# Second attention: each head's stack on 64 partitions, one score matmul per head, one run for the value product

## The reference

```
loc_p   = softmax(Qb Kb^T / 4);                 out  = loc_p Vb
cross_p = softmax(Qb Kw^T / 4), Kw = own, left and right block;  out += cross_p Vw
```

## Time and profile before

| | |
|---|---|
| median of three runs | 1000.9 us |
| lowest, highest run | 999.47, 1026.03 us |
| span of the profiled execution | 999.6 us |
| mean granted clock of TensorE | 0.915 of 2.4 GHz |
| instructions | 15908 |
| busy: TensorE, VectorE, ScalarE, GpSimd | 852.5, 444.8, 351.0, 227.6 us |
| second attention | between 84 and 501 us, with attention 1 of batches 1 to 3 between the passes |
| experts | from about 530 us to the end |

### The profile page before, as it was taken

One profiled execution on the slowest core, in us unless ns is written; L12 is line 12 of the kernel. 1 busy time (PEld: TensorE's weight loads), 2 busy tenths in 40 slices (PEclk: granted clock), 3 DMA queues, 4 the chain that ended last, 5 costly groups with the idle time before them and its releaser, 6 DMA issues. The chain is left out here.

```text
span 999.6 us, 15908 instructions
## 1 busy us (share of the span) xinstructions
PE 852.5 (85%) x5062; PEld 643.2 (64%) x5063; DVE 444.8 (45%) x821; ACT 351.0 (35%) x902; POOL 227.6 (23%) x248
## 2 busy tenths in 40 slices
PE   3476779987997899799994999899999999999940
PEld 3365566766675757565674999767766677777630
DVE  5854537556756675544236655222222222222216
ACT  1210126442643354314515443033333333333313
POOL 6730203020302030000002577511111111111115
PEclk9687689989998899895897999999999999999975
DMA  9702120212021204120008211544111111111025
GB/s 306 127 0 66 50 57 4 60 53 61 4 58 48 66 0 129 34 55 1 4 1 314 103 53 53 142 167 135 31 37 31 31 31 31 37 31 32 26 73 196
DMA packets 59000, 68.48 MB, mean 69 GB/s; under 512 B 18160, under 2 KB 43632, under 8 KB 58832
## 3 DMA queue, kind: packets, MB, share of 16 engines
q1 hardware_dynamic: 55552, 58.61, 20.1%
q0 software_dynamic: 3408, 9.34, 2.6%
HBM read 38.23 MB, written 16.59 MB: 55 GB/s over the span
## 5 line engine op out<-in xcount | busy, mean ns | idle before, releaser
L1529 PE MATMUL ps<-we,hT 128*128 x624 | 142.8, 382 | 2.5 <-ACT hT L714 2.5
L1509 PE MATMUL ps<-we,xT 128*128 x312 | 142.3, 599 | 1.9 <-issue 1.9
L1529 PEld LDWEIGHTS ps<-we,hT 128*128 128x128 f32 x624 | 119.7, 192 | 35.5 <-issue 20.9
L918 DVE TENSOR_REDUCE mx<-ps 128x4 f32<-128x512 f32 (+1 forms) x128 | 102.9, 822 | 77.0 <-PE ps L1349 76.0
L1112 DVE COPY hp<-ps 128x512 f32<-128x512 f32 x78 | 50.3, 686 | 160.1 <-PE ps L1509 160.1
L714 ACT ACTIVATE hT<-ps,b1T 128x128 f32<-128x128 f32 x312 | 84.7, 383 | 37.2 <-PE ps L1520 37.2
L1509 PEld LDWEIGHTS ps<-we,xT 128*128 128x128 f32 x312 | 56.8, 192 | 59.2 <-issue 59.2
L1349 PE MATMUL ps<-k_stack,q_stack 96*128 96x256 f32 (+1 forms) x256 | 76.7, 389 | 18.7 <-DMA q_stack<-q_s 11.7
L617 ACT ACTIVATE pT<-ps 128x256 f32<-128x256 f32 x128 | 49.1, 384 | 107.9 <-PE ps L1364 100.3
L540 ACT ACTIVATE xT<-ps 128x256 f32<-128x256 f32 x39 | 14.8, 383 | 180.8 <-PE ps L1492 180.8
L1349 PEld LDWEIGHTS ps<-k_stack,q_stack 96*128 96x128 f32 x256 | 43.5, 212 | 52.6 <-issue 24.4
(11 more groups left out here) (202 smaller groups left out, 1339.1 us busy)
## 6 DMA issues: line engine op xcount, KB each, us to landing
we<-in_w SPq DMA_DIRECT2D x16, 1024.0 KB
k_stack<-k_s SPq DMA_DIRECT2D x96, 64.0 KB, 2.0
q_stack<-q_s SPq DMA_DIRECT2D x192, 32.0 KB, 2.0
slot_rows<-attn SPq DMA_DIRECT2D x1, 4992.0 KB, 21.2
xs<-slot_rows SPq DMA_DIRECT2D x39, 128.0 KB, 2.1
yl<-pair_out SPq DMA_DIRECT2D x4, 1024.0 KB, 9.2
x_raw<-in_xT SPq DMA_DIRECT2D x4, 512.0 KB, 3.9
X<-in_x SPq DMA_DIRECT2D x4, 512.0 KB, 7.2
```

The lines of the kernel that those rows point to most:

```text
L918: nc.vector.tensor_reduce(mx[:, n, 2 * p:2 * p + 2, r0:r0 + nb], ps[:, 2 * (u % 2):2 * (u % 2) + 2, 0:nb * P].rearrange("p h (b k) -> p h ...
L1509: m = nc.tensor.matmul(ps[:, 2 + c, :], xT[:, q, k, :], w[:, bass.ds(e, 1), k * HID + c * 512:k * HID + (c + 1) * 512].rearrange("p o n -> ...
L1529: m = nc.tensor.matmul(ps[:, 6, 0:D], hT[:, c, :], w[:, bass.ds(e, 1), KD * HID + c * D:KD * HID + (c + 1) * D].rearrange("p o n -> p (o n)"),
```

## The change

Each head gets a stack of its own of 64 partitions: head 0 of a pair stands on partitions 0 to 63, head 1 on 64 to 127. 48 rows hold the three products (16 each). Rows 48 to 55 hold the local difference, two rows for each of the four blocks, each filled for its own query block and zero elsewhere; `k_stack` has ones there only for the key block of the same number. Rows 56 and 57 hold the window's maximum against ones. So the right correction is added for local and side blocks by the same matmul, and for each head one matmul over the whole window (256 or 384 columns) takes the place of the shared local one and the shared sides one. The maxima matmuls contract 48 rows, the probability ones 58, in place of 96, 98 and 100.

`q_stack` has half the size. The columns of the query and key weights of attention 2 are reordered on the host, so that a copy takes 32 partitions of source into 16 partitions and two pairs: 12 issues of 64 KB for each of two groups of pairs, 24 for a half. TensorE waits for a group at every eighth unit, not for a pair at every fourth. `aug_rows` has 10 issues: for each head of a pair one for the window rows and four for the local ones. The fixed rows of `k_stack` come from a small tile `k_rows`, which GpSimd makes with a memset and two selects, by two DMAs at the start of SP's order; VectorE's memset goes.

The value product has one run of four matmuls for a block of keys, over its whole window, in odd units only. Even key blocks go to bank 7 and odd ones to bank 6, so that a query block's own part and its neighbours' part are in different banks; `turn_out` picks them accordingly. The exponentials have 256 or 384 columns each, one per head, and the second matmul of a unit waits for the second exponential of the unit before.

```diff
-PAIR_DMAS = 3 + 2 * 3
-
-
-def side_blocks(i):
-    return [n for n in (i - 1, i + 1) if 0 <= n < NT]
+GROUPS = 2
+GROUP_DMAS = 2 * 3 * 2
+ROWS_A = 3 * DH
+ROW_LOC = ROWS_A
+ROW_CROSS = ROW_LOC + 2 * NT
+ROWS_B = ROW_CROSS + 2
+AUG_DMAS = 2 + 2 * NT
+
+
+def window(i):
+    return max(i - 1, 0), 3 if 0 < i < NT - 1 else 2
...
-        q_stack = sb("q_stack", [P, HEADS, S], FR, att)
+        q_stack = sb("q_stack", [P, HEADS // 2, S], FR, att)
...
+            sp.wait_ge(s["k_set"], 3)
+            for j in range(2):
+                sp.dma_start(k_stack[64 * j + ROW_LOC:64 * j + ROWS_B, :, :].bitcast(F),
+                             k_rows[:, :].unsqueeze(1).broadcast_to([2 * NT + 2, HEADS // 2, S])).then_inc(s["k_ones"], 16)
...
-                for g in range(PAIRS):
-                    for sec, part in enumerate((0, 1, 0)):
-                        sp.dma_start(k_stack[32 * sec:32 * sec + 32, h * PAIRS + g, :].bitcast(F),
-                                     k_s[32 * g:32 * g + 32, h, part, :].bitcast(F)).then_inc(stacked[g], 16)
-                    for head in (2 * g, 2 * g + 1):
+                for g in range(GROUPS):
+                    pairs = slice(h * PAIRS + 2 * g, h * PAIRS + 2 * g + 2)
+                    for j in range(2):
+                        rows = slice(64 * j + 32 * g, 64 * j + 32 * g + 32)
+                        for sec, part in enumerate((0, 1, 0)):
+                            r = 64 * j + DH * sec
+                            sp.dma_start(k_stack[r:r + DH, pairs, :].bitcast(F),
+                                         k_s[rows, h, part, :].bitcast(F)).then_inc(stacked[g], 16)
                         for sec, part in enumerate((0, 0, 1)):
-                            r = 32 * sec + 16 * (head % 2)
-                            sp.dma_start(q_stack[r:r + 16, h * HALF + head, :].bitcast(F),
-                                         q_s[16 * head:16 * head + 16, h, part, :].bitcast(F)).then_inc(stacked[g], 16)
+                            r = 64 * j + DH * sec
+                            sp.dma_start(q_stack[r:r + DH, pairs, :].bitcast(F),
+                                         q_s[rows, h, part, :].bitcast(F)).then_inc(stacked[g], 16)
 
             def aug_rows(b, h):
                 sp.wait_ge(s["augT_out"], 2 * b + h + 1)
-                for r in range(4):
-                    sp.dma_start(q_stack[96 + r:97 + r, h * HALF:(h + 1) * HALF, :].bitcast(F),
-                                 augT[r * HALF:(r + 1) * HALF, :].bitcast(F)).then_inc(s["aug_in"], 16)
+                pairs = slice(h * PAIRS, (h + 1) * PAIRS)
+                for j in range(2):
+                    at = j * 4 * PAIRS
+                    r = 64 * j + ROW_CROSS
+                    sp.dma_start(q_stack[r:r + 2, pairs, :].bitcast(F),
+                                 augT[at:at + 2 * PAIRS, :].bitcast(F)).then_inc(s["aug_in"], 16)
+                    for n in range(NT):
+                        r = 64 * j + ROW_LOC + 2 * n
+                        sp.dma_start(q_stack[r:r + 2, pairs, n * P:(n + 1) * P].bitcast(F),
+                                     augT[at + 2 * PAIRS:at + 4 * PAIRS, n * P:(n + 1) * P].bitcast(F))\
+                            .then_inc(s["aug_in"], 16)
...
+            nc.gpsimd.memset(k_rows[:, :], 1.0).then_inc(s["k_set"], 1)
+            k_blocks = k_rows[:, :].rearrange("r (n k) -> r n k", k=P)
+            pool.wait_ge(s["k_set"], 1)
+            nc.gpsimd.affine_select(out=k_blocks, in_=k_blocks, compare_op=ALU.is_ge, fill=0.0,
+                                    base=0, pattern=[[-2, NT], [0, P]], channel_multiplier=1).then_inc(s["k_set"], 1)
+            pool.wait_ge(s["k_set"], 2)
+            nc.gpsimd.affine_select(out=k_blocks[0:2 * NT], in_=k_blocks[0:2 * NT], compare_op=ALU.is_ge, fill=0.0,
+                                    base=1, pattern=[[2, NT], [0, P]], channel_multiplier=-1).then_inc(s["k_set"], 1)
...
-                        w = 2 * P * len(side_blocks(i))
+                        w = P * window(i)[1]
                         bank = 2 if a is None and u % 2 else 4
                         at = 2 * UNITS * c + 2 * u
-                        act.wait_ge(s["b_ps"], at + 1)
                         if m >= 2:
                             act.wait_ge(s["pv_done"], 8 * c + m - 1)
-                        nc.scalar.activation(pT[:, m % 2, u % 2, 0:2 * P], ps[:, bank, 256:512], ACT.Exp, scale=SCALE2)\
-                            .then_inc(s["b_exp"], 1)
-                        act.wait_ge(s["b_ps"], at + 2)
-                        nc.scalar.activation(pT[:, m % 2, u % 2, 2 * P:2 * P + w], ps[:, bank + 1, 0:w], ACT.Exp,
-                                             scale=SCALE2).then_inc(s["b_exp"], 1)
+                        for j in range(2):
+                            act.wait_ge(s["b_ps"], at + j + 1)
+                            nc.scalar.activation(pT[:, m % 2, u % 2, j * w:(j + 1) * w], ps[:, bank + j, 0:w], ACT.Exp,
+                                                 scale=SCALE2).then_inc(s["b_exp"], 1)
...
-            nc.vector.memset(k_stack[96:P, :, :].bitcast(F), 1.0).then_inc(s["k_ones"], 1)
...
-                dve.wait_ge(s["pv_done"], 8 * c + 4 * g + 4)
+                dve.wait_ge(s["pv_done"], 8 * c + 4 * g + 3)
...
-                def pv_local(m):
+                def pv(m):
                     g, i = m // NT, m % NT
-                    pe.wait_ge(s["b_exp"], 2 * (UNITS * c + 2 * m + 2) - 1)
-                    if i == 0 and (full or g):
-                        pe.wait_ge(s["oc_out"], 2 * c + g)
+                    k0, nb = window(i)
+                    bank = 7 - i % 2
+                    pe.wait_ge(s["b_exp"], 2 * (UNITS * c + 2 * m + 2))
+                    if i < 2 and (full or g):
+                        pe.wait_ge(s[("os_out", "oc_out")[i]], 2 * c + g)
                     for j in range(4):
-                        nc.tensor.matmul(ps[32 * j:32 * j + 32, 6, i * P:(i + 1) * P],
-                                         v_aug[:, i, hc * HALF + 4 * g + j, :],
-                                         pT[:, m % 2, j // 2, (j % 2) * P:(j % 2 + 1) * P],
-                                         start=True, stop=True, skip_group_check=True)
-
-                def pv_sides(m):
-                    g, i = m // NT, m % NT
-                    sides = side_blocks(i)
-                    pe.wait_ge(s["b_exp"], 2 * (UNITS * c + 2 * m + 2))
-                    if i == 0 and (full or g):
-                        pe.wait_ge(s["os_out"], 2 * c + g)
-                    w = len(sides) * P
-                    for j in range(4):
-                        out = ps[32 * j:32 * j + 32, 7, :].rearrange("p (n q) -> p n q", q=P)[:, sides[0]:sides[-1] + 1:2, :]
-                        last = nc.tensor.matmul(
-                            out, v_aug[:, i, hc * HALF + 4 * g + j, :],
-                            pT[:, m % 2, j // 2, 2 * P + (j % 2) * w:2 * P + (j % 2 + 1) * w].rearrange("p (n q) -> p n q", q=P),
-                            start=i == 0, stop=True, skip_group_check=True)
+                        last = nc.tensor.matmul(ps[32 * j:32 * j + 32, bank, k0 * P:(k0 + nb) * P],
+                                                v_aug[:, i, hc * HALF + 4 * g + j, :],
+                                                pT[:, m % 2, j // 2, (j % 2) * nb * P:(j % 2 + 1) * nb * P],
+                                                start=i < 2, stop=True, skip_group_check=True)
                     last.then_inc(s["pv_done"], 1)
 
                 if c is not None:
-                    pe.wait_ge(s["k_ones"], 1)
-                    pe.wait_ge(s["aug_in"], 64 * (c + 1))
+                    pe.wait_ge(s["k_ones"], 32)
+                    pe.wait_ge(s["aug_in"], 16 * AUG_DMAS * (c + 1))
                 for u in range(UNITS):
                     if a is not None:
                         p, n = u // NT, u % NT
-                        k0, nb = max(n - 1, 0), 3 if 0 < n < NT - 1 else 2
-                        if n == 0:
-                            pe.wait_ge(stacked[p], 16 * PAIR_DMAS * (a + 1))
+                        k0, nb = window(n)
+                        if n == 0 and p % 2 == 0:
+                            pe.wait_ge(stacked[p // 2], 16 * GROUP_DMAS * (a + 1))
                         if u >= 2:
                             pe.wait_ge(s["a_red"], UNITS * a + u - 1)
                         for j in range(2):
+                            rows = slice(64 * j, 64 * j + ROWS_A)
                             m = nc.tensor.matmul(ps[:, 2 * (u % 2) + j, 0:nb * P],
-                                                 q_stack[0:96, ha * HALF + 2 * p + j, n * P:(n + 1) * P],
-                                                 k_stack[0:96, ha * (HALF // 2) + p, k0 * P:(k0 + nb) * P],
+                                                 q_stack[rows, ha * PAIRS + p, n * P:(n + 1) * P],
```

(37 more changed lines are left out.)

29 lines of the change are left out of this document (17 added, 12 removed).

## The result

The kernel after the change takes 1021.64 us (median of four runs, 1018.37 to 1024.82); the kernel before, run beside it, 1008.97 us (four runs, 999.47 to 1026.03). The ratio is 1.0194 with a 95% interval of 1.0149 to 1.0239: slower by 1.5 to 2.4%, where 985 us was forecast. Whether it is more than 2% is open.

The account below looks back on a forecast made before the run. TensorE was taken to bound passes 1 to 7. Start -1.2, pass 0 -7.0, stacks -5.5, loops +3.4, pass 7 -3.8 and pass 8 -1.9 sum to -16.0: from 999.6, plus 1.3, 985 us; range 966 to 1021.

Parts of the forecast that it names:

- the loops: Passes 1 to 6: two units take 2.49 instead of 2.42 us at 2.4 GHz, +3.4 us in all.
- the stacks: Passes 2, 4 and 6: fewer issues end TensorE's waits for stacks, -5.5 us in sum, between -2 and -10.
- rival 2: Clock falls in passes 1 to 6, from fewer contracted rows and TensorE idling in odd units: 1036 us, chance 0.20.
- Overlap of the halves: Score matmuls on the array's two halves: none assumed, by the weight loads; side by side the period would be 2.36 us.
- The wait chain: Odd units: the second probability matmul waits for ScalarE's exp, which uses up the value run's saving; +0.56 us a pass.
- Pass 0: 24 instead of 36 issues land stacks sooner and end GpSimd's last operation earlier: -7.0 us, between -3 and -8.
- The later stacks: Passes 2, 4, 6: later stacks, six more aug issues and a first group of 12 issues cost +1.0 us together.
- Pass 7 and 8: Pass 7, at the low clock throughout: -3.8 us; pass 8: -2.9 us from its units, -1.9 with its late maxima rows.
- the late rows: Pass 8's maxima rows come by 10 issues instead of 4 and land 1.0 us behind the pass's start.
- Start: Before pass 0: q_stack halves (-3.46 us), GpSimd gets a memset and two selects (about 2.2): -1.2 us, between +1 and -6.
- Rival 3: Stack copies: an issue of 64 KB costs double, 1.25 us, so stacks take 30 us: 1030 us, chance 0.03.

Follow-up runs that it names:

- e2: The change with both heads' score matmuls on the first head's rows (0 to 47, 0 to 57), so none can overlap: 1044.42 us, one run.
- e3: The kernel before with all its score matmuls cut to rows 0 to 47, low parts mostly and maxima left out: 1064.81 us, one run.
- e8: e1 with only the maxima matmuls cut to 48 rows, the probability matmuls staying at 106: 1065.95 us, one run.
- e12: e9 with only the probability matmuls cut to rows 0 to 57 of 106, the maxima staying at 96: 1039.73 us, one run.
- e1: The change without its 64-partition tiles: both heads share 96 rows again, q_stack full size, all else kept: 979.83 us, ratio 0.9803 to the kernel before.
- e11: The change, 64-row tiles kept, with the value run split so that each unit has one: 1008.34 us, one run.
- e9: e1 with the ws load issued behind the last body's first stack and 24 instead of 16 keep_clock matmuls ahead of pass 8: 973.02 us, ratio 0.9719.
- e5: e1 with the value run cut by columns into two, so that each unit has one: 993.11 us, ratio 1.0056 to the kernel before.
- e6: e1 with 36 instead of 24 DMA issues per stack, the q rows copied pair by pair: 999.34 us, ratio 1.0085 to the kernel before.

## Why the prediction was wrong, step by step

**The step that failed** is the one that priced passes 1 to 6 at 2.4 GHz. The forecast had them at +3.4 for the loops and -5.5 for the stacks, -2.1 together. They came out at +28.4 (19.8 + 8.6), at a granted clock of 0.50 to 0.61, and another 7.4 us lie between the passes, 4.6 of them the wait ahead of pass 6. The range took in three fallen passes; all six fell. It is rival 2, at 0.20, and of its two reasons the first (48 and 58 rows instead of 96 and 100) holds by e2, e3, e8 and e12, the second (idle time in the odd unit) doesn't, by e1 with the wait at 1.00 and e11 without it at 0.53. The Trainium skill, TensorE: Matmul & The Clock Gate, in its section on psum-queue depth-cycling, names short idle times between groups of matmuls as what makes the clock swing; these traces don't show that here, with 1.00 where the wait stood (e1) and 0.53 where it didn't (e11). Against rival 2 I had set pass 8, which holds its clock with waits in it. That row could speak of waits only: pass 8 before contracts 100 rows. No row of before spoke of rows, and I weighted the case as if one did. Its price for two units at the low clock, 3.65 us, met the 3.61 measured (value runs from 144.36 to 162.41, five periods) partly by luck, for it left out the overlap: without it e2 has 3.87 (150.18 to 165.65, four periods). 51 us on top of the forecast gave 1036, and the change took 1021.6: the low clock cost the six passes 37 us against e1 and e9, not 42, the stacks of passes 2, 4 and 6 are worth 6.7 us more than forecast (below), start and pass 0 gave 3.4 more, and the stages between the passes grew by 7.4 us, the wait included, not by 9.

**Overlap of the halves.** Wrong: I took the start distance of the weight loads in the earlier trace rows as evidence against it, but those two loads name 96 rows each, more than a half, so the row says nothing of loads on different halves. The Trainium skill, TensorEngine Tiling (Array Packing), Key Properties, says that different tiles load and multiply in parallel; the trace agrees (two loads in 0.29 us at the low clock where e2 needs 0.50; a maxima pair in 0.22 us at the high one, 137.34 to 137.56). At the low clock the overlap gave back 1.5 to 1.7 us a pass (e2). What the change would take with its overlap at 2.4 GHz was never seen: no kernel with such tiles held the clock through a pass.

**The wait chain.** Right in mechanism and size: +0.56 us a pass was forecast, and e1 against e5 shows 0.5 to 0.6. At the low clock it is 2.2 to 2.7 (e11). That answers where the merged value run's gain went: TensorE saved the streaming and then waited for ScalarE.

**Pass 0.** -7.0 forecast, -7.9 measured, by the steps named: 24 issues in 15.8 us (15.1 forecast), GpSimd's last operation 12.0 us earlier, 4.3 of them because the stack itself began earlier, and with it VectorE's subtraction. One wait of 1.86 us for the second group stayed, which I had put at nothing. e6 shows that the issues bring all of it: 7.3 to 7.5 us, counted from SP's first stack issue.

**Stacks in passes 2, 4, 6.** The term was too small. In e9, at the high clock, these passes take 20.86, 20.86 and 21.41 us against 24.78, 24.64 and 24.18 before: -10.5, where -5.5 and three times +0.56 come to -3.8. I had left 2.8 us in each for the turn of `aug` behind GpSimd; it waits 0.3 us. In the change this gain lies under the clock. The later stacks stood at +1.0 in all in the forecast; ahead of pass 6 alone they brought a wait of 3.98 us, with the `ws` load in front of them.

**Pass 7 and 8.** Pass 7 up to the start of pass 8 went from 40.5 to 35.1 us, -5.4 against -3.8 and +1.0 for the late rows. Pass 8 went from 14.8 to 14.4, not by 2.9; 3.5 us of it ran at the low clock (508.3 to 511.8). In e1, at the high clock throughout, it has 13.25 us, so the term was twice too large without the clock too. The sum of both passes, -5.7, is the forecast's, by errors that cancel. In e1 pass 7 stayed high, 10.2 us less up to pass 8, where I had -12 as the bound. How often pass 7 of the kernel before falls isn't known; one execution is traced.

**Start.** -1.2 forecast, -3.7 measured. VectorE's operation fell from 9.99 to 6.30 us, as the memset did from 6.93 to 3.50; GpSimd made `k_rows` before that and held nobody up. But over the runs pass 0 starts at 80.0 to 86.3 us in the four kernels with the half-size `q_stack`, and at 83.2 to 90.2 in those with the full one, so the difference of two executions proves little here.

**Rival 3** (a 64 KB issue costs double) is out: 0.62 us each (1.86 us for three).
